# A four-layer graph network on one core: the four engines' orders set anew, row sums and a normalization moved

## Time and profile before

| | us |
|---|---|
| median of 3 runs | 1447.32 (1446.82 to 1449.07) |
| the profiled execution | 1446.77 |
| its span | 1445.0 |
| PE busy | 1385.2 (96%) |
| PEld busy | 1300.0 (90%) |
| DVE busy | 1368.0 (95%) |
| ACT busy | 1233.1 (85%) |
| POOL busy | 1014.0 (70%) |

### The profile page before, as it was taken

How to read it: one execution, slowest core, us unless ns; L and a number is a source line. 1 busy time by engine, 2 the same in 40 slices (tenths; PEclk the granted TensorE clock), 3 DMA queues, 4 the chain that set the end, 5 groups by cost and what they waited for, 6 DMA issues and landing times.

```text
span 1445.0 us, 45699 instructions
## 1 busy us (share of the span) xinstructions
PE 1385.2 (96%) x14092; PEld 1300.0 (90%) x14092; DVE 1368.0 (95%) x6094; ACT 1233.1 (85%) x3911; POOL 1014.0 (70%) x1684
## 2 busy tenths in 40 slices
PE   4999999999999999999999999999999999999986
PEld 4888999999999999999999999999999999999975
DVE  3899999999999999999999999999999999999986
ACT  5889988988988888889888889889888889889854
POOL 5577767777777777777777777777777777777663
PEclk9999999999999999999999999999999999999999
DMA  3000100101100101100001000000001001001001
GB/s 113 17 17 17 31 17 31 31 17 31 31 17 31 31 17 31 31 17 31 30 18 31 26 22 31 26 22 31 24 24 31 22 25 31 21 27 31 13 20 37
DMA packets 38112, 39.76 MB, mean 28 GB/s; under 512 B 2416, under 2 KB 37488, under 8 KB 37872
## 3 DMA queue, kind: packets, MB, share of 16 engines
q1 hardware_dynamic: 37872, 36.84, 8.1%
HBM read 20.05 MB, written 16.78 MB: 25 GB/s over the span
## 4 chain that ended last, share of the span: by engine, by line
DVE 47%; PE 32%; issue 16%; POOL 2%; ACT 1%; DMA 0%; DVEq 0%; POOLq 0%; SPq 0%; ACTq 0%
PE bank L330 12%; DVE stats L749 9%; DVE s_prod L802 8%; PE mid L330 7%; PE mid L374 4%; PE bank L386 4%; DVE x L881 4%; DVE masked L759 3%; DVE x_exp L871 3%; DVE x L897 3%; DVE o L900 3%; DVE m_t_lo L817 2%; PE bank L540 2%; DVE o_gam L793 2%; DVE mean_var L753 2%
## 5 line engine op out<-in xcount | busy, mean ns | idle before, releaser
L583 ACT ACTIVATE probs<-masked,neg_max 128x128 f32<-128x128 f32 x1024 | 397.7, 395 | 30.0 <-DVE neg_max L759 30.0
L759 DVE CUSTOM_DVE_ANT_0 masked<-mid,mask 128x128 f32<-128x128 f32 x1024 | 226.9, 287 | 11.4 <-issue 11.4
L802 DVE CUSTOM_DVE_ANT_0 s_prod<-h,wa_rows 128x256 f32<-128x256 f32 x256 | 198.2, 826 | 2.9 <-issue 2.9
L583 ACT ACTIVATION_READ_ACCUMULATOR probs<-masked,neg_max 128x1 f32 x1024 | 198.2, 194 | 0.0
L749 DVE BATCH_NORM_STATS2 stats<-x 128x6 f32<-128x256 f32 x384 | 143.1, 413 | 0.2
L365 PE MATMUL bank<-ident,probs 128*128 128x128 f32 x1024 | 139.7, 274 | 2.5 <-POOL probs L984 1.2
L975 POOL TENSOR_TENSOR xb<-x,b_proj_beta 128x512 f32<-128x512 f32 x64 | 82.5, 1290 | 81.4 <-DVE o_res L875 81.4
L955 POOL TENSOR_TENSOR var_eps<-mean_var,eps 128x2 f32<-128x2 f32 x192 | 43.0, 224 | 137.0 <-DVE mean_var L753 137.0
L958 POOL TENSOR_TENSOR rstd<-var_eps,minus_half 128x2 f32<-128x2 f32 x192 | 133.3, 694 | 0.0
L365 PEld LDWEIGHTS bank<-ident,probs 128*128 128x128 f32 x1024 | 114.2, 140 | 10.9 <-POOL probs L984 1.6
L970 POOL TENSOR_TENSOR h_t_lo<-h_t_full,h_t_hi 128x512 fp32r<-128x512 f32 x64 | 81.8, 1278 | 45.1 <-ACT h_t_hi L645 45.1
(11 more groups left out here) (157 smaller groups left out, 5983.6 us busy)
## 6 DMA issues: line engine op xcount, KB each, us to landing
x<-in_x SPq DMA_DIRECT2D x64, 256.0 KB, 2.8
out_x<-x SPq DMA_DIRECT2D x64, 256.0 KB, 2.2
w_qkv_sb<-in_w_qkv SPq DMA_DIRECT2D x1, 768.0 KB, 5.2
w_v_sb<-in_w_v_t SPq DMA_DIRECT2D x1, 256.0 KB, 5.4
w_proj_sb<-in_w_proj SPq DMA_DIRECT2D x1, 256.0 KB, 5.8
w_q_sb<-in_w_q SPq DMA_DIRECT2D x1, 256.0 KB, 6.4
w_k_sb<-in_w_k SPq DMA_DIRECT2D x1, 256.0 KB, 7.0
w_gat_x<-in_w_gat SPq DMA_DIRECT2D x1, 256.0 KB, 5.8
```

The costliest lines, as they stand in the source:

```text
L583: last = act.activation(probs[:, r, s], masked[:, r, s], ACT.Exp, scale=-1.0, bias=neg_max[:, r, s:s + 1], accum_out=sums[:, r, s:s + 1])
L759: last = dve.tensor_tensor_reduce(out=masked[:, r, s], in0=mid[:, r, s * N:(s + 1) * N], in1=mask[:], scale=1.0, scalar=LARGE, op0=ALU.add ...
L802: last = dve.tensor_tensor_reduce(out=s12_prod[:, b, j], in0=h2[:, i5, b], in1=wa_rows[:, j], scale=1.0, scalar=0.0, op0=ALU.mult, op1=ALU ...
```

## The change

The diff rewrites the order in every engine's `step`, renames which bank each accumulator takes, and makes three further edits: z1 is computed by ScalarE, with a shift from GpSimd, as z0 is; some operations move from one step to the next (the stage number in `on[...]` says so); and set-up work moves with them.

VectorE's step after: moments of o, relu_lo, e_neg_max, x2_exp, o_gam, x2, inv_sums 2-3, x1, moments of x2, moments of x1, att_norm, x3_up, y_t_lo, moments of x0, rel, moments of x3, masked 0 and 1, o_t_lo, row sums, m_t_lo, sum_sq, masked 2 and 3, x4, o_res, o, inv_sums 0-1.

GpSimd's step after: product 2, roots of x1, roots of x2, rel_sq, roots of x0, roots of x3, x3b, h_t_lo, inv_norm, xb, e_mask, product 1, root of o, product 0, product 3.

ScalarE's step after: m_t_hi, z0, h_t_hi and h_t1_full, exponentials 0 and 1, e_leaky, h_t0, h3, u_exp, exponentials 2 and 3, att, g_t, k_t, v1, v0, probs_t 1, q_t, y_t_hi, probs_t 0, 3, 2, att_t, z1, h2, o_t_hi.

TensorE's step after: heads, m, z1's transposes, v, sum_sq, y, o, z0's transposes, s2, u, v1, rel_v, g, probs 1, k, q, y_t, probs 0, rel, probs 3, probs 2, att, scores.

The diff, cut to its core:

```diff
-        z0_bank = bank4[:]
+        z0_bank = bank6[:]
...
-        z1_bank = mid[:, 1]
+        z1_bank = mid[:, 0]
...
-        rel_bank = bank7[:]
+        rel_bank = bank6[:]
...
-        u_bank = bank5[:]
+        u_bank = mid[:, 2]
...
 sync
-                pb, p_out = t - 2, t - 8
+                pb, p_out = t - 1, t - 8
...
 tensor, step
+                if on[3]:
+                    pe.wait_ge(z_ready[1], done(p3))
+                    bank_free(pe, (max_ready[0], p1, 1), (probs_t_ready[0], p2, 1), (g_ready, p4, 1),
+                              (e_leaky_ready, p6, 2))
+                    transposes(z1_bank, z[1]).then_inc(h_t_psum[1], 1)
...
+                if on[6]:
+                    pe.wait_ge(m_lo_ready, done(p6))
+                    bank_free(pe, (max_ready[2], p1, 1))
+                    rows(halves(u_bank), m_t_p, w_gat_p, 0, D).then_inc(u_psum, 1)
...
-            run(pe, step, [(0, first_weights), (0, value_weights), (1, fold), (3, folded_weights),
-                          (1, next_weights), (5, last_weights), (2, wa_rows_made)])
+            run(pe, step, [(0, first_weights), (1, value_weights), (1, fold), (3, folded_weights),
+                          (2, next_weights), (6, last_weights), (4, wa_rows_made)])
...
 scalar, step
+                if on[2]:
+                    act.wait_ge(shift_ready[1], done(p2))
+                    wait_before(act, h_t_psum[1], p2)
+                    for b in range(2):
+                        last = act.activation(z[1][:, b], x1[:, i2, b], ACT.Identity, bias=shift[1][:, b:b + 1],
+                                              scale=rstd[:, 1, b:b + 1])
+                    last.then_inc(z_ready[1], 1)
...
 vector, step
+                if on[7]:
+                    dve.wait_ge(u_exp_ready, done(p7))
+                    dve.scalar_tensor_tensor(x2_exp[:], u_exp[:], 1.0, x2[:, i7], ALU.min, ALU.add).then_inc(x2_exp_ready, 1)
...
                 if on[2]:
                     dve.wait_ge(probs_ready[2], done(p2))
                     dve.wait_ge(probs_ready[3], done(p2))
                     dve.reciprocal(inv_sums[:, 2:4], sums[:, 2:4]).then_inc(inv_sums_ready[1], 1)
                 if on[3]:
+                    dve.wait_ge(o_gam_ready, done(p3))
+                    dve.wait_ge(o_res_ready, done(p3))
+                    dve.wait_ge(ln_rstd[LN_O], done(p3))
+                    if p3 > 1:
+                        dve.wait_ge(x2_ready, done(p3 - 2, 2))
+                    for b in range(2):
+                        dve.scalar_tensor_tensor(x1[:, i3, b], o_gam[:, b], rstd[:, LN_O, b:b + 1], o_res[:, b],
+                                                 ALU.mult, ALU.add).then_inc(x1_ready, 1)
...
-                if on[3]:
-                    normalize(1, p3, x1[:, i3])
                 if on[2]:
                     dve.wait_ge(o_hi_ready, done(p2))
 ...
+                if on[5]:
+                    dve.wait_ge(h2_ready, done(p5))
+                    wait_before(dve, e_leaky_ready, p5, 2)
+                    dve.memset(s12_turn[:], 0.0)
+                    for b in range(2):
+                        for j in range(2):
+                            last = dve.tensor_tensor_reduce(out=s12_prod[:, b, j], in0=h2[:, i5, b], in1=wa_rows[:, j], scale=1.0, scalar=0.0,
+                                                            op0=ALU.mult, op1=ALU.add, accum_out=s12[:, b, j:j + 1])
+                    last.then_inc(s12_ready, 1)
...
 gpsimd, step
-                if on[3]:
-                    wait_before(pool, z_ready[1], p3)
-                    inverse_root(1, p3)
+                if on[3]:
+                    wait_before(pool, z_ready[1], p3)
+                    inverse_root_and_shift(1, p3, shift[1]).then_inc(shift_ready[1], 1)
```

More of the change, by code:

```diff
@@ L431, in step @@
                 i0, i1, i2, i3, i4, i5, i6, i7, i8 = [(par + s) % 2 for s in range(STREAMS)]
+                if on[2]:
+                    for r in range(RG):
+                        pe.wait_ge(probs_t_ready[r], done(p2))
+                    pe.wait_ge(v0_ready, done(p2))
+                    bank_free(pe, (probs_t_ready[2], p2, 1), (probs_t_ready[1], p2, 1), (o_ready, p3, 1))
+                    heads_times_values().then_inc(heads_psum, 1)
+                if on[6]:
+                    pe.wait_ge(att_t_ready, done(p6))
+                    pe.wait_ge(h2_ready, done(p6))
+                    bank_free(pe, (probs_t_ready[3], p2, 1), (v1_ready, p4, 1))
+                    for c in range(C):
+                        for b in range(2):
+                            last = pe.matmul(m_bank[:, (c * 2 + b) * N:(c * 2 + b + 1) * N], h2[:, i6, b, c * 128:(c + 1) * 128],
+                                             att_t[:, b], start=True, stop=True)
+                    last.then_inc(m_psum, 1)
@@ new lines, in step @@
+                if on[4]:
+                    pe.wait_ge(rel_sq_ready, done(p4))
+                    for b in range(2):
+                        last = pe.matmul(rel_bank[:, 256 + b:257 + b], rel_sq[:, b], ones[:, 0:1], start=True, stop=True)
+                    last.then_inc(sum_sq_psum, 1)
+                if on[8]:
+                    pe.wait_ge(y_lo_ready, done(p8))
+                    bank_free(pe, (max_ready[1], p1, 1), (y_lo_ready, p8, 1), (x2_ready, p5, 2))
+                    rows(halves(y_bank), y_t_p, w_out_p, 0, D).then_inc(y_psum, 1)
@@ new lines, in step @@
+                if on[2]:
+                    pe.wait_ge(o_lo_ready, done(p2))
+                    bank_free(pe, (o_lo_ready, p2, 1), (probs_t_ready[2], p2, 1), (probs_t_ready[1], p2, 1))
+                    for b in range(2):
+                        last = product(o_bank[:, b * D:(b + 1) * D], o_t_p, w_proj_p,
+                                       lambda a, c: a[:, b, c], lambda a, c: a[:, c])
+                    last.then_inc(o_psum, 1)
+                if on[0]:
+                    pe.wait_ge(z_ready[0], done(p0))
+                    bank_free(pe, (sum_sq_ready, p4, 1), (k_ready, p1, 1))
+                    transposes(z0_bank, z[0]).then_inc(h_t_psum[0], 1)
@@ L448, in step @@
[L448 to L453, removed]
                 if on[3]:
                     pe.wait_ge(h_lo_ready[1], done(p3))
[L456 to L459, removed]
+                    bank_free(pe, (e_leaky_ready, p5, 2), (h1_full_ready, p3, 1), (max_ready[0], p1, 1),
+                              (probs_t_ready[0], p2, 1))
@@ L472, in step @@
[L472 to L480, removed]
@@ L492, in step @@
                     last.then_inc(y_t_psum, 1)
[L493 to L498, removed]
-                if on[1]:
[L500 to L505, removed]
+                if on[1]:
+                    pe.wait_ge(probs_norm_ready[0], done(p1))
+                    bank_free(pe, (g_ready, p3, 1), (e_leaky_ready, p5, 2), (h1_full_ready, p3, 1),
+                              (max_ready[0], p1, 1))
+                    transpose_probs(0).then_inc(probs_t_psum[0], 1)
                 if on[3]:
@@ L515, in step @@
+                if on[5]:
+                    pe.wait_ge(att_norm_ready, done(p5, 2))
+                    bank_free(pe, (v0_ready, p1, 1))
+                    for b in range(2):
+                        last = pe.transpose(att_bank[:, b * N:(b + 1) * N], att_norm[:, b], ident[:])
+                    last.then_inc(att_t_psum, 1)
                 if on[0]:
[L516 to L519, removed]
@@ L533, in step @@
[L533 to L536, removed]
-                if on[3]:
[L538 to L548, removed]
-                    transposes(z1_bank, z[1]).then_inc(h_t_psum[1], 1)
@@ L550, in step @@
[L550 to L559 removed]
+                    bank_free(pe, (probs_t_ready[0], p1, 1), (g_ready, p3, 1), (e_leaky_ready, p5, 2),
+                              (h1_full_ready, p3, 1))
@@ L664, in step @@
                     exps(2).then_inc(probs_ready[2], 1)
+                    act.wait_ge(max_ready[3], done(p1))
+                    wait_before(act, probs_t_psum[3], p1)
+                    exps(3).then_inc(probs_ready[3], 1)
+                if on[5]:
+                    act.wait_ge(e_max_ready, done(p5))
+                    wait_before(act, att_norm_ready, p5, 2)
+                    for b in range(2):
+                        act.activation(att[:, b], e_mask[:, b], ACT.Exp, bias=e_neg_max[:, b:b + 1],
+                                       accum_out=att_sum[:, b:b + 1]).then_inc(att_ready, 1)
@@ L784, in step @@
                 i0, i1, i2, i3, i4, i5, i6, i7, i8 = [(par + s) % 2 for s in range(STREAMS)]
-                if on[2]:
-                    dve.wait_ge(probs_ready[2], done(p2))
-                    dve.wait_ge(probs_ready[3], done(p2))
-                    dve.reciprocal(inv_sums[:, 2:4], sums[:, 2:4]).then_inc(inv_sums_ready[1], 1)
+                if on[3]:
+                    dve.wait_ge(o_ready, done(p3))
+                    moments(LN_O, p3, o)
+                if on[1]:
```

(48 more changed lines are left out.)

452 lines of the change are left out of this document (196 added, 256 removed).

## The result

| | before | after |
|---|---|---|
| median, us | 1447.36 (1446.82 to 1449.07) | 1499.72 (1497.88 to 1500.91) |
| profiled span, us | 1445.0 | 1497.7 |
| one steady step, us | 21.70 | 22.52 |

The ratio is 1.0361, with a 95% interval of 1.0349 to 1.0373: slower by 52 us. Of the 52.7 us between the spans, the 56 full steps bring 56 x (22.52 - 21.70) = 46, the sixteen part steps the other 7.

The account below looks back on a forecast made before the run. VectorE with its waits was to bound the step: 18.95 + 2.1 + 0.9 + 0.4 = 22.4 us, 0.7 more than before. Over 56 full steps that adds 40 to 1446.8, giving 1487, or 1488 on the median's footing; range 1415 to 1540.

Parts of the forecast that it names:

- VectorE's own work: VectorE's list in a steady step, without the new collisions: 18.95 us, down from 21.70.
- z1's 0.65: z1 leaving VectorE for ScalarE: saves VectorE 0.65 us a step.
- Row sums against x3b and h_t_lo: VectorE's row sums, 3.6 us after rel, wait for GpSimd's x3b, then h_t_lo: 2.1 us a step together.
- the second wait: h_t_lo, queued behind x3b, lets one row sum pass and shuts out the next: about 1.06 us.
- x1: VectorE's x1 pair against GpSimd's products 3 and 2; product 3 gets in between: 0.9 us more a step.
- x_exp: VectorE's x_exp waits for GpSimd's product 1: 0.4 us a step, between 0 and 0.8.
- o_gam free: VectorE's o_gam comes after x_exp and ends just before GpSimd's product 0 starts, so no wait.
- TensorE's own 20.7: TensorE's own work in a steady step without its visible stops: 20.7 us, between 20.20 and 21.49.
- The part steps: The 16 steps without all nine streams: fewer old and new collisions, -15 to +15 us, taken as 0.
- The rule by which powers block too: GpSimd's powers would make VectorE's o_gam and att_norm each wait up to 0.69 us; step up to 23.8.
- The fast rival: Row sums miss x3b and h_t_lo, TensorE leads with 20.7 us a step, kernel takes 1391 us; chance 0.15.

Follow-up runs that it names:

- e5: The changed kernel with z1 computed by VectorE again instead of ScalarE; 1537.1 us, ratio 1.0622 to the kernel before.
- e1: The changed kernel with x3b moved on GpSimd from before h_t_lo to behind inv_norm, in two buffers; 1406.1 us, ratio 0.9714 to the kernel before.
- e4: The changed kernel with the row sums as plain one-source reductions, product with folded weights left out; 1401.4 us, ratio 0.9686 to the kernel before.
- e2: The changed kernel with x1 put before the reciprocal inv_sums 2-3 on VectorE; 1457.0 us, ratio 1.0056 to the kernel before.
- e3: The changed kernel with both x3b moved behind inv_norm and x1 put before the reciprocal; 1389.5 us, ratio 0.9598 to the kernel before.
- e6: e3 with z1 computed by VectorE again instead of ScalarE; 1392.2 us, ratio 0.9624 to the kernel before.
- e8: The changed kernel with x3b as a one-source copy on GpSimd, added constant left out; 1406.7 us, ratio 0.972 to the kernel before.

## Why the prediction was right

It gave 1488 us, range 1415 to 1540; measured were 1499.7. By its steps:

- **VectorE's own work, 18.95.** Step 22.52, less the waits measured below (2.18 + 0.87 + 0.49), is 18.98. e5 confirms z1's 0.65 with 0.63.
- **Row sums against x3b and h_t_lo, 2.1.** The four take 3.56 (733.06 to 736.62) against 1.38: 2.18. The place, 3.6 us after rel, was right: 729.49 + 3.57 = 733.06, and x3b came at 733.10. e1 and e4 show that these waits are the cause. The way to the second wait was not as predicted: h1 was to be there by 4.5, so that h_t_lo would be queued when x3b ended, but GpSimd waited 0.39 for it and h_t_lo came at 5.53. It still shut out the fourth row sum, since the third was in work until 735.25. Had h1 come some 0.25 later yet (an estimate, 735.25 less 735.02), h_t_lo would have found the fourth in work and let it end, so this half of the 2.1 had some luck in it.
- **x1, 0.9.** 723.14 to the next start at 724.78 is 1.64, clean 0.77: 0.87. e2 gave 0.74 a step back.
- **x_exp, 0.4.** 1.10 start to start against 0.61: 0.49.
- **o_gam free.** It ends before product 0 starts (0.87; in before it takes 0.83).
- **TensorE's own 20.7.** e3 shows 20.68, with TensorE never idle.
- **The part steps, taken as 0,** were the term most off: they cost 7 us. The prediction had looked in them for collisions and for waits for the set-up, and taken both as 0; what the runs show is that the new order's first m_t_lo comes 8 us later (109.01 against 100.89). The other 6 us of the difference to 1499.7 is a step of 22.52 where 22.4 had been summed.
- The rule by which powers block too would have given up to 23.8 us a step. At 744.08 a power of 0.82 stands beside the o_gam pair of 0.87: no wait of its length, as the trace of before had it.
- The fast rival, the change does what it says, named as its condition that x3b ends before the row sums start and h_t_lo comes after them. e1 fulfils this condition in another way and lands at 1406 where the rival had 1391; e3, with x1's wait gone too, lands at 1389. (The two bounds that the prediction gives beside the 1391 are 1 us low: 56 x 1.5 and 56 x 0.21 off 1447.3 leave 1363 and 1435.)

What stays open is which wait in the first steps makes the new order fill up 8 us later.

## What to carry to other kernels

A busy instruction can be a waiting one. Compare the shortest and the longest duration of one shape before believing an engine's busy share: here 1.5 against 0.42, and 3.5 us of a step of 22.5. When VectorE instructions with two SBUF sources share the time with GpSimd, list every wide GpSimd instruction, sums, differences and copies too, and place both lists from a common event; keeping clear of one kind alone moves the wait to the next. Then ask which engine leads once the waits are gone, as e6 against e5 shows: the same edit is worth 37 us or 3.

## What was not expected of the hardware

GpSimd and VectorE took turns at the row sums: a GpSimd instruction that came while a row sum was in work waited for its end (x3b 1.53 and h_t_lo 1.38 against 1.29 in e1, the copy of e8 0.86 against 0.61), and the next row sum then waited for nearly the whole of it (1.08 us), even when it stood right behind. So four short instructions met by two long ones wait twice, not once. And removing the first of two meetings removed the second with it.
